# Eight row normalisations inside a long two-layer program: loops on VectorE against straight code in quarters on VectorE and ScalarE

## What is computed

```python
def _layernorm(x, axis=-1, eps=1e-05):
    m = jnp.mean(x, axis=axis, keepdims=True)
    v = jnp.var(x, axis=axis, keepdims=True)
    return (x - m) / jnp.sqrt(v + eps)
...
x = x + _L0_attn_a_ref(_layernorm(x, axis=-1), ...)   # recurrence over 2048 steps
x = x + _L0_ffn_ref(_layernorm(x, axis=-1), ...)      # slots ("ffn1")
x = x + _L0_attn_b_ref(_layernorm(x, axis=-1), ...)   # mixing
x = x + _L0_ffn_ref(_layernorm(x, axis=-1), ...)      # slots ("ffn2")
x = x + _L1_attn_a_ref(_layernorm(x, axis=-1), ...)   # long convolution
x = x + _L1_ffn_ref(_layernorm(x, axis=-1), ...)      # ternary ("ffn3")
x = x + _L1_attn_b_ref(_layernorm(x, axis=-1), ...)   # attention
x = x + _L1_ffn_ref(_layernorm(x, axis=-1), ...)      # ternary ("ffn4")
```

## Time and profile before

| | us |
|---|---|
| median of three runs | 14836.72 |
| lowest, highest | 14822.92, 14843.74 |
| the profiled execution | 14818.84 |
| span from first to last instruction in it | 14816.9 |
| VectorE busy | 10244.3 |
| ScalarE busy | 8213.0 |
| TensorE busy | 6600.0 |

### The profile page before, as it was taken

How to read it: one execution, slowest core, us unless ns; L and a number is a source line. 1 busy time by engine, 2 the same in 40 slices (tenths; PEclk the granted TensorE clock), 3 DMA queues, 4 the chain that set the end, 5 groups by cost and what they waited for, 6 DMA issues and landing times. The chain is left out here.

```text
span 14816.9 us, 232336 instructions
## 1 busy us (share of the span) xinstructions
PE 6600.0 (45%) x53605; PEld 4592.0 (31%) x53605; DVE 10244.3 (69%) x54621; ACT 8213.0 (55%) x42324; POOL 866.4 (6%) x824
## 2 busy tenths in 40 slices
PE   6222222222222222222222222246776567688887
PEld 5222222222222222222222222233444344333335
DVE  4777777777777777777777777763853983365551
ACT  4666666666666666666666666652642111133331
POOL 0000000000000000000000000000000861200000
PEclk8555555555555555555555555557996778789999
DMA  1000000000000000000100000000000000201110
GB/s 49 12 18 12 15 16 12 18 12 18 13 18 12 18 12 18 12 18 13 18 13 18 12 18 12 17 8 11 0 1 22 0 0 6 61 10 21 24 19 17
DMA packets 336648, 233.28 MB, mean 16 GB/s; under 512 B 23221, under 2 KB 319873, under 8 KB 335110
## 3 DMA queue, kind: packets, MB, share of 16 engines
q1 hardware_dynamic: 335366, 219.56, 7.9%
HBM read 193.64 MB, written 25.43 MB: 15 GB/s over the span
## 5 line engine op out<-in xcount | busy, mean ns | idle before, releaser
L515 PE MATMUL scan_p_car<-scan_hs,scan_mean_mat 32*32 32x2 f32 x16392 | 578.0, 198 | 6858.6 <-DVE scan_hb L642 6846.2
L515 PEld LDWEIGHTS scan_p_car<-scan_hs,scan_mean_mat 32*32 32x32 f32 x16392 | 402.1, 135 | 7037.5 <-DVE scan_hb L642 7025.0
L560 ACT ACTIVATE scan_act_ps<-scan_act_ps 128x64 f32<-128x64 f32 (+1 forms) x8193 | 1641.7, 200 | 64.6
L560 ACT ACTIVATE scan_act_ps<-scan_r 128x64 f32<-128x64 f32 x2048 | 466.2, 228 | 1869.9 <-DVE scan_r L639 1869.9
L542 PE MATMUL scan_p_y<-scan_c_masked,scan_hb 128*64 128x4 f32 x16384 | 1234.1, 253 | 0.0
L520 PE MATMUL scan_p_car<-scan_eps_row,ones 1*128 1x3 f32 x4102 | 1198.1, 360 | 38.7 <-DMA scan_a_log<-L_attn_a_A_log 38.5
L2378 DVE TENSOR_REDUCE attn_top_pieces<-attn_ps 128x1 f32<-128x512 f32 (+3 forms) x1440 | 824.0, 606 | 563.3 <-PE attn_ps L2261 325.4
L560 ACT ACTIVATE scan_cm<-scan_dl,scan_s 128x64 f32<-128x64 f32 x2049 | 712.1, 348 | 737.4 <-DVE scan_s L665 737.4
L542 PEld LDWEIGHTS scan_p_y<-scan_c_masked,scan_hb 128*64 128x64 f32 x16384 | 1055.4, 216 | 34.8
L639 DVE TENSOR_TENSOR scan_c<-scan_V,scan_cm 128x64 f32<-128x64 f32 x4096 | 739.8, 221 | 460.7 <-ACT scan_cm L560 413.5
L520 PEld LDWEIGHTS scan_p_car<-scan_eps_row,ones 1*128 1x128 f32 x4102 | 1020.2, 307 | 71.5 <-DMA scan_a_log<-L_attn_a_A_log 38.9
(11 more groups left out here) (451 smaller groups left out, 19876.9 us busy)
## 6 DMA issues: line engine op xcount, KB each, us to landing
scan_step_in<-scan_scratch SPq DMA_DIRECT2D x520, 256.0 KB, 6.1
attn_qT<-qk_scratch SPq DMA_DIRECT2D x60, 256.0 KB, 9.3
attn_kT<-qk_scratch SPq DMA_DIRECT2D x60, 256.0 KB, 18.7
qk_scratch<-qkv_parts SPq DMA_DIRECT2D x32, 384.0 KB, 2.5
scan_scratch<-prep_dts SPq DMA_DIRECT2D x32, 256.0 KB, 2.1
x<-L_attn_a_x SPq DMA_DIRECT2D x1, 4096.0 KB
out<-x SPq DMA_DIRECT2D x1, 4096.0 KB
filter_taps<-c_kT SPq DMA_DIRECT2D x1, 2048.0 KB
```

The costliest lines, as they stand in the source:

```text
L515: last = nc.tensor.matmul(p_car[slot][rows, 0:2], mean_mat[rows, :], hs[rows, :], start=False, stop=True)
L560: nc.scalar.activation(dst, src, func, **kw).then_inc(counts[par]["act"], 1)
```

## The change

The normalisation becomes straight code in four quarters of eight tiles. VectorE takes the statistics and aggregates of quarters 0 and 1, then, for each quarter, a small product shift = -mean * root and every other tile of tensor_scalar, and after it the statistics and aggregates of the quarter two ahead. ScalarE takes the roots of each quarter as eight columns, one quarter ahead, normalises the other tiles with an Identity of scale root and bias shift, and copies the transposed groups of the quarter before. xn now holds all 32 tiles, or is the slot layer's own array, so GpSimd has no copy to make, and TensorE waits for no buffer but the PSUM pair.

The argument `measured` says that the statistics are there already, in an array ln_stats that lives through the program. It is set for ffn1 and for ln_q. They are taken by VectorE in the phase before, in scan_output_phase and in ternary_phase, one bn_stats behind each addition to x and a wait for that addition. The ternary phase does so for ffn3 and for ffn4; behind ffn4 no normalisation follows.

```diff
-        xn = ph.sb("xn", [P, 2, G, D])
+        xn = ph.sb("xn", [P, NT, D]) if natural is None else natural
...
+                def moments(q):
+                    if not measured:
+                        for t in quarter(q):
+                            nc.vector.bn_stats(stats[:, t, :], x[:, t, :]).then_inc(stats_done, 1)
+                    for t in quarter(q):
+                        if not measured:
+                            dve.wait_ge(stats_done, t + 1)
+                        nc.vector.bn_aggr(mv[:, t, :], stats[:, t, :]).then_inc(mv_done, 1)
+                def normalized(q):
+                    tiles = slice(q * QT, (q + 1) * QT)
+                    dve.wait_ge(rstd_done, q + 1)
+                    nc.vector.scalar_tensor_tensor(shift[:, tiles], mv[:, tiles, 0], -1.0, rstd[:, tiles], ALU.mult, ALU.mult).then_inc(shift_done, 1)
+                    for t in quarter(q)[0::2]:
+                        nc.vector.tensor_scalar(xn[:, t, :], x[:, t, :], mv[:, t, 0:1], rstd[:, t:t + 1], ALU.subtract, ALU.mult).then_inc(xn_vector, 1)
...
+                def normalized(q):
+                    act.wait_ge(shift_done, q + 1)
+                    for t in quarter(q)[1::2]:
+                        nc.scalar.activation(xn[:, t, :], x[:, t, :], ACT.Identity, scale=rstd[:, t:t + 1], bias=shift[:, t:t + 1]).then_inc(xn_scalar, 1)
...
+                for g in range(GROUPS):
+                    if g >= 2:
+                        pe.wait_ge(tp_free, g - 1)
+                    pe.wait_ge(xn_vector, (g + 1) * (G // 2))
+                    pe.wait_ge(xn_scalar, (g + 1) * (G // 2))
...
@@ scan_output_phase (in ternary_phase the same with n * GP + g + GP + 1)
                         nc.vector.tensor_tensor(xt, xt, p_o[s][:, 0:D], ALU.add).then_inc(added, 1)
+                        dve.wait_ge(added, i * 2 + s + 3)
+                        dve.sem_inc(taken, 1)
+                        nc.vector.bn_stats(env["ln_stats"][:, bass.ds(i * 2 + s, 1), :], x[:, bass.ds(i * 2 + s, 1), :]).then_inc(measured, 1)
```

More of the change, by code:

```diff
@@ L110, in _ @@
             def _(dve):
[L111 to L130, removed]
@@ L132, in _ @@
+                moments(0)
+                moments(1)
+                for q in range(QUARTERS):
+                    normalized(q)
+                    if q + 2 < QUARTERS:
+                        moments(q + 2)
             @block.scalar
@@ L134, in _, with roots @@
                 nc.scalar.preload_act_table_set(EXP_LN)
[L135 to L145, removed]
+                def roots(q):
+                    tiles = slice(q * QT, (q + 1) * QT)
+                    act.wait_ge(mv_done, (q + 1) * QT)
+                    nc.scalar.activation(lnv[:, tiles], mv[:, tiles, 1], ACT.Ln, bias=env["ln_eps"][:, 0:1]).then_inc(ln_done, 1)
+                    act.wait_ge(ln_done, q + 1)
+                    nc.scalar.activation(rstd[:, tiles], lnv[:, tiles], ACT.Exp, scale=-0.5).then_inc(rstd_done, 1)
@@ L147, in _ @@
+                roots(0)
+                for q in range(QUARTERS):
+                    if q + 1 < QUARTERS:
+                        roots(q + 1)
+                    normalized(q)
+                    for g in range(max(q - 1, 0) * PER_Q, q * PER_Q):
+                        turned(g)
+                for g in range((QUARTERS - 1) * PER_Q, GROUPS):
+                    turned(g)
             @block.tensor
             def _(pe):
[L149 to L169, removed]
+                for g in range(GROUPS):
[3 more added lines that the diff above has]
+                    pe.wait_ge(xn_scalar, (g + 1) * (G // 2))
+                    for k in range(KD):
+                        for t in range(g * G, (g + 1) * G):
+                            last = nc.tensor.transpose(tp[g % 2][k][:, (t % G) * P:(t % G + 1) * P], xn[:, t, k * P:(k + 1) * P], env["ident"][:, :])
+                    last.then_inc(tp_done, 1)
@@ L742, in scan_output_phase @@
         loaded, yt_done, o_done, added = ph.sem("loaded"), ph.sem("yt_done"), ph.sem("o_done"), ph.sem("added")
+        taken, measured = ph.sem("taken"), ph.sem("measured")
         with nc.Block() as block:
@@ L2486, in attention_layer @@
 def attention_layer(nc, env):
-    layernorm_phase(nc, env, "ln_q")
+    layernorm_phase(nc, env, "ln_q", measured=True)
     env["attended"] = env["xnT"][:, :, :].rearrange("p k t -> p (k t)").rearrange("p (n d) -> p n d", d=D)
@@ L2554, in program @@
         env["qk_scratch"] = nc.dram_tensor("qk_scratch", (2, B, PARTS, D, T), BF16, kind="Internal").ap()
-        phases = [load_phase, recurrence_layer, slot_layer("ffn1"), mixing_layer, slot_layer("ffn2"), convolution_layer,
-                  ternary_layer("ffn3"), attention_layer, ternary_layer("ffn4"), store_phase]
+        phases = [load_phase, recurrence_layer, slot_layer("ffn1", measured=True), mixing_layer, slot_layer("ffn2", measured=False), convolution_layer,
+                  ternary_layer("ffn3", measured=False), attention_layer, ternary_layer("ffn4", measured=False), store_phase]
         for phase in phases:
```

46 lines of the change are left out of this document (25 added, 21 removed).

## The result

The changed kernel takes **14722.92 us** (median of 4 runs, 14712.52 to 14751.5) against 14840.23 us (4 runs) for the kernel before: ratio 0.9926, 95% interval 0.9908 to 0.9943. The forecast was 14771 us with a range from 14738 to 14805. The direction was right; the time lies 48 us under the forecast and 15 us under the range. Its profiled execution took 14722.81 us.

The account below looks back on a forecast made before the run. It took a line of phases with barriers to bound the kernel, mostly the VectorE-ScalarE recurrence; gains of 41.3 and 29.8 us in the normalisations less 5.4 for sums, 65.7 off the 14836.7 median, gave 14771 us, range 14738 to 14805.

Parts of the forecast that it names:

- The stages' working order: Normalisations: VectorE works 15.6 us, then ScalarE takes roots, Identities and copies; 26.0 us before turns in stages without ready sums.
- 0.50 a tile: Normalisations: one ScalarE Identity of 128x256 takes 0.50 us, taken from the convolution; bounds 0.40 and 0.52.
- two such turns: End of each normalisation: ScalarE idles while TensorE transposes groups 6 and 7, 0.8 or 2.5 us a stage by clock level.
- More than forecast: Rival: TensorE at upper level in all normalisations (10 us), Identities at 0.40 (8 us), 18 us run-to-median gap; 14743 us; chance 0.13.
- The price of the sums: Output and ternary phases: early statistics cost 0.65 us plus 4.8 us for two ternary layers, total 5.4 us.
- Half of it: Rival: in six normalisations VectorE slows by 1.34 beside ScalarE's reads, losing 32 us; 14803 us; chance of part gain 0.18.
- The early sums do nothing: Rival: statistics in ternary and output phases hold up TensorE, taking back 62 us; 14833 us; chance of no change 0.09.
- GpSimd copy: In ffn1 and ffn2 its removal ends VectorE's slowdown, 3.3 us, already inside the two gains and not added.
- The change does not touch it: The recurrence, about 9.5 ms of VectorE and ScalarE chain, was taken as unaffected by the change.
- unchanged within some us: Sign to look for: the recurrence's time stays the same within some us.
- The rival on code loading: Rival: the normalisations' straight code stalls VectorE 3.1 us a time, four per stage, 99 us; 14870 us; chance 0.05.

Follow-up runs that it names:

- second comparison: Both kernels rerun unchanged: the changed kernel took 14729.53 us (12 runs), the kernel before beside it 14832.65 us (29 runs), ratio 0.9943.
- pads: Kernel before plus dummy load-phase instructions: 247 VectorE memsets, ratio 0.9974; 22 ScalarE activations, 1.0; 39 TensorE matmuls, 0.9999; all three, 0.9982.
- six placements: VectorE breaks at 127 (kernel before), 8 (before plus 247 memsets), 6 (changed), 125, 63, 13 (changed plus 9, 71, 121 memsets); scans 9530.9 to 9573.9 us.

## Why the prediction was wrong, and where it was right

1. **The stages' working order** held. ScalarE's idle before the first roots is 2.04 us, four Identities take 2.06, VectorE is done 8 us early, and in none of the eight windows does VectorE or ScalarE wait without a releaser. Its 0.50 a tile, taken for an Identity from another phase, was right.
2. **The term "two such turns"** was mis-sized. It stood at 0.8 us for two stages and 2.5 for the six others, because four or more of the old groups had run at TensorE's lower level. (In ffn1 before, the third to fifth group had run at 1.00 and the last three at the lower level again, so "after four or more" was loosely read there.) Measured, there is in the last two quarters one such wait in most stages, of 0.20 us in ln_m, 0.38 in ffn2 and 0.51 in ffn3, and two in ln_a (0.21 and 0.41) and ln_q (0.20 and 0.47). The lower level itself was there, as argued. The first six groups of ln_m, its last two, and the first six of ffn1:

```profile
10215.40:10229.70 14.30, 10.12 (x48) 9.08 (x48) 10.03 (x46) 12.17 (x28) 0.00 (x0) 0.63 0.01 2
10230.10:10232.30 2.20, 2.07 (x16) 1.71 (x16) 0.00 (x0) 2.00 (x6) 0.00 (x0) 1.00 0.00 0
10001.70:10013.60 11.90, 10.59 (x48) 9.82 (x48) 5.23 (x31) 11.84 (x28) 0.00 (x0) 0.50 0.01 1
```

But those six groups hide behind ScalarE's own work, and when the last two came, the granted clock had risen: over the transposes of the last two it is 0.99 or 1.00 in four of the eight stages and 0.91, 0.86, 0.77 and 0.75 in ffn2, ffn3, ln_a and ln_q. The forecast charged the level of the early groups to the late ones. And mostly only one of the two is late: group 6 waits for the copies of group 4, as argued, and group 7 is turned while ScalarE copies group 6. Stages with statistics took 26.1 to 26.6 (forecast 26.8 and 28.5), the two others 19.0 and 19.6 (21.3). That is 14 us of the 48, and the rival "More than forecast" named it.
3. **The price of the sums**: 5.3 us against 5.4. The wait on itself is 0.24 us, the tail 4.04 us (4.1 forecast), and the statistics hide in the output phase as argued, where VectorE still waits 71.8 us for TensorE.
4. **"Half of it"**: no. TENSOR_SCALAR keeps 1.38 us for four beside ScalarE's Identities. **"The early sums do nothing"**: no, but on balance they give only 8 us by the rows. The **GpSimd copy** went with its cost: ffn2 is now 26.24 us beside ln_m's 26.06, where the two stood at 36.37 and 33.05.
5. **The step that failed outright** is "The change does not touch it", said of the recurrence, with "unchanged within some us" at the end. It was 11.7 us shorter in the first pair of traces and 20 to 23 in the repeated ones, through the place of VectorE's code. The rival on code loading came nearest, at the wrong place and with the wrong sign: it priced breaks in the new straight code and took the 3.1 us at the back edge as given. One break, of 0.22 us, had been seen in ln_c, and the same trace had 240 like it on the longest chain of the program. The view that shows it is the list of the step lengths, of which the earlier trace rows give only the sum at the back edges.
6. **The rest.** Forecast 14771, less 14 for the turns, 2 for the gaps and 21 for the scan, is 14734. The last 11 us to 14723 are not in one place (taken from the two profiled executions, -95.9 against -65.7 is 30 us more, of which the stages are 14 and the scan 11.7; the other 18 of the 48 are the distance of before's profiled execution from its median): outside the stages and the scan, attention moved by +12 and all else by -16 between the two profiled executions. The 18 us by which the profiled execution of before lay under its median did not recur either; the one of after lies at its median. In the second comparison, whose medians are 14832.65 and 14729.53, the same terms give 14832.65 - 65.7 - 14 - 2 - 21 = 14730. That this meets the median is in part luck, as the 10 us of attention (below) and the rest outside are not in it. A range that takes the scatter of untouched phases as nil was too narrow. The prediction also had a slip: the rival "More than forecast" names 10, 8 and 18 us, which is 36 and gives 14735, and took off 28. And the bracket of "More" began at 14730 where the range ended at 14738.

Left open: attention took 1528 to 1538 us in seven traces of the old code (with pads or without) and 1537 to 1547 in seven of the new. That is some 10 us the other way, and no run here tells why.

## What to carry to other kernels

In a long unrolled loop on one engine's chain, read the lengths of the steps and not only their median: breaks at equal distances in the instruction stream cost something only where they meet the chain, so an edit to that engine's code ahead of the loop can move its time by 43 us in 9570 (9530.9 to 9573.9) without touching it. Before a small gain is put down to an edit, compare the phases it doesn't touch; and such a loop can be placed, here with 71 memsets beside an input transfer, though the 16 us that this took off the scan did not show in the kernel's median over five runs. Behind an addition that its engine waits for anyway, a statistic is free; at a phase's end, or where that engine sets the pace, it is paid in full.

## What the runs showed of the hardware

- VectorE had breaks at every 128th instruction that the trace records, through a written-out body of 7279: up to 0.31 us on the chain, in every pass at the same place. They moved with VectorE's code in six placements, record for record. The Trainium skill (Runtime: NRT & Kernel Launch, Instruction fetch mechanics) has code fetched in blocks of 256 instructions and calls the crossing mostly hidden. Here 26 of the 56 crossings of a pass were hidden in the kernel before and 48 in the changed one. The distance of 128 and the cost are what the traces show; that fetching is the cause is an inference, as no record names it.
- A taken back edge cost VectorE 3.0 to 3.5 us. Where the next boundary was 6 or 8 records behind its target it waited 1.8 to 2.7 us more; at 13 records 1.1 us more (7.7 us in 7), of which 0.7 show in the step.
- 22 activations on ScalarE left the scan at 9569.5 us. With 39 matmuls on TensorE its breaks stayed too (9574.4 us, by the median step).
- In one and the same phase TensorE was granted its upper level early or late in different traces: 142 us or 163 and 173. ln_m's eight groups of transposes are another case: 0.63 on average in the first six, 1.00 in the last two.
